# Wide attention of a block chain: the sums of four heads in one matmul visit, their reciprocals spread by ScalarE, and the output quarters a period later

## What is computed

```python
def cross_attention(x, ctx, wq, wk, wv, wo, bo):
    q, k, v = ...                       # 20 heads of 64
    scores = einsum('bhnd,bhmd->bhnm', q, k) * SCALE
    attn = softmax(scores, axis=-1)
    out = einsum('bhnm,bhmd->bhnd', attn, v)
    return einsum('bnf,fe->bne', out, wo) + bo

x = cross_attention(layer_norm(x, g1, be1), layer_norm(x, g1, be1), wq1, wk1, wv1, wo1, bo1) + x
x = cross_attention(layer_norm(x, g2, be2), context, wq2, wk2, wv2, wo2, bo2) + x
```

## Time and profile before

| | us |
|---|---|
| median of 3 runs | 3481.67 (3481.03 to 3483.08) |
| the profiled execution | 3482.07 |
| its span | 3480.3 |
| TensorE busy | 3284.0 |
| VectorE busy | 1760.0 |
| ScalarE busy | 1505.8 |
| GpSimd busy | 672.0 |
| granted clock, mean share of full | 0.985 |

### The profile page before, as it was taken

The page is one execution under the profiler, slowest core; times in us unless marked ns, Lnnn a source line. Parts: engine busy times, 40 slices in busy tenths (PEclk is TensorE's granted clock), DMA queues, the critical chain, the costliest instruction groups (busy, mean ns, idle before and its releaser), DMA issues.

```text
span 3480.3 us, 39327 instructions
## 1 busy us (share of the span) xinstructions
PE 3284.0 (94%) x15478; PEld 1478.6 (42%) x15478; DVE 1760.0 (51%) x2728; ACT 1505.8 (43%) x2023; POOL 672.0 (19%) x420
## 2 busy tenths in 40 slices
PE   7999999999999999998999899999997999989997
PEld 3434344443434343434454344444433455643443
DVE  2645455454545455562223666777771221656774
ACT  3544444444454545451111555666652111326664
POOL 2433334333334343340000000000000000000000
PEclk9999999999999999999999999999999999989999
DMA  3000000000100000002000000000003000000000
GB/s 109 20 16 19 17 16 19 22 15 22 32 16 19 16 22 13 16 7 59 0 1 25 1 1 1 22 9 7 1 1 83 0 1 22 3 5 6 5 1 31
DMA packets 43558, 60.54 MB, mean 17 GB/s; under 512 B 7408, under 2 KB 31216, under 8 KB 43376
## 3 DMA queue, kind: packets, MB, share of 16 engines
q1 hardware_dynamic: 43376, 58.02, 5.8%
HBM read 55.39 MB, written 2.62 MB: 17 GB/s over the span
## 4 chain that ended last, share of the span: by engine, by line
PE 86%; ACT 6%; DVE 5%; issue 2%; DMA 0%; POOL 0%; SPq 0%; ACTq 0%; DVEq 0%; POOLq 0%
PE bank L548 8%; PE bank L465 8%; PE bank L1027 6%; PE bank L670 5%; PE bank L350 5%; PE bank L606 4%; PE bank L1463 4%; PE bank L960 4%; PE bank L1465 4%; PE bank L1143 3%; PE bank L609 3%; PE bank L642 3%; PE bank L1466 2%; PE bank L1080 2%; PE bank L1168 2%; DVE heads L985 2%
## 5 line engine op out<-in xcount | busy, mean ns | idle before, releaser
L498 DVE TENSOR_REDUCE heads<-bank 128x2 f32<-128x1024 f32 x320 | 392.4, 1226 | 673.7 <-PE bank L487 673.7
L985 DVE TENSOR_REDUCE heads<-bank 128x1 f32<-128x512 f32 x960 | 597.9, 683 | 237.2 <-PE bank L973 236.4
L521 ACT ACTIVATE probs<-bank 128x1024 f32<-128x1024 f32 x320 | 327.7, 1024 | 130.1 <-PE bank L474 129.9
L534 POOL TENSOR_TENSOR heads<-heads,probs 128x1024 f32<-128x1024 f32 x160 | 377.1, 2357 | 12.5
L530 POOL TENSOR_TENSOR heads<-probs 128x1024 f32<-128x1024 f32 x80 | 192.4, 2405 | 931.9 <-ACT probs L521 931.9
L465 PE MATMUL bank<-heads 64*128 64x512 f32 x1280 | 335.7, 602 | 0.1
L960 PE MATMUL bank<-heads 32*128 32x512 f32 x1920 | 296.5, 628 | 25.7 <-ACT weights L998 14.9
L548 PE MATMUL bank<-probs,values 128*64 128x512 f32 x1280 | 292.3, 598 | 9.3 <-ACT heads L617 4.9
L577 DVE RECIPROCAL rec<-ox 128x128 f32<-128x128 f32 x320 | 270.2, 907 | 8.0 <-ACT ox L570 8.0
L998 ACT ACTIVATE weights<-bank 128x1024 f32<-128x1024 f32 x238 | 230.6, 1021 | 100.2 <-PE bank L960 99.6
L1487 ACT ACTIVATE probs<-bank,b_col 128x512 f32<-128x512 f32 x80 | 55.0, 687 | 455.3 <-PE bank L1466 455.3
(11 more groups left out here) (199 smaller groups left out, 4725.2 us busy)
## 6 DMA issues: line engine op xcount, KB each, us to landing
heads<-in_wqk SPq DMA_DIRECT2D x40, 320.0 KB, 2.9
heads<-in_wqk SPq DMA_DIRECT2D x40, 256.0 KB, 2.6
ctx_in<-in_ctx SPq DMA_DIRECT2D x12, 384.0 KB, 3.7
weights<-in_L_xattn_wo SPq DMA_DIRECT2D x2, 1600.0 KB, 11.7
x_res<-in_x SPq DMA_DIRECT2D x4, 640.0 KB, 12.3
out<-x_res SPq DMA_DIRECT2D x1, 2560.0 KB, 8.7
weights<-in_L_xattn_w_ff SPq DMA_DIRECT2D x1, 1600.0 KB, 12.3
weights<-in_L_xattn_ff_w SPq DMA_DIRECT2D x1, 1600.0 KB, 14.2
```

Source lines behind the costliest of these rows:

```text
L498: nc.vector.tensor_reduce(v["negm"][:, U % 2, qb, :].rearrange("p (g k) -> p g k", g=2)[:, :, 0], M.ROWS[:, :, :], AX.X, ALU.max, negate=T ...
L521: nc.scalar.activation(v["probs"][:, kb, :, :], M.COLS[kb % 2][:, :, :], ACT.Exp, scale=float(r.work[n][0].prm["dh"]) ** -0.5).then_inc(r. ...
L534: nc.gpsimd.tensor_tensor(ps, ps, pr[:, k, :, :], ALU.add).then_inc(r.sem("part"), 1)
L985: nc.vector.tensor_reduce(v["negm"][:, tile, qb, 32 * h + at:32 * h + at + 1], r.bank_of(item, m)[:, :], AX.X, ALU.max, negate=True).then_ ...
```

## The change

The sums are made once in two periods, in the odd ones. Four matmuls of 32 columns put the sums of the pair of the even period in rows 0 to 31 and 64 to 95 of the bank, those of the odd one in rows 32 to 63 and 96 to 127. ScalarE evicts this tile once, and VectorE takes its reciprocals once, in the following even period. In the odd period after that ScalarE makes two tiles of it, `rec` for the even pair and `rec_odd`, in which each sum stands in all 64 rows of its head: a copy of the whole tile, two copies of 32 rows, and when they have landed two more of 32 rows (`w_spread_act`). Then VectorE multiplies both pairs' mixes (`w_divide_dve`). Since the last division of a batch is now in period 1 of the next, the output quarters move from periods 1 to 4 to periods 2 to 5, and V2 from periods 5 and 6 to periods 0 and 1. `step_items` is changed in the same way.

```diff
@@ -176,6 +176,7 @@
+                v["rec_odd"] = M.heads[:, 9984:10496]
...
@@ -451,7 +452,7 @@
-                    items += [(f"mix{u}", n), (f"den{u}", n)]
+                    items += [(f"mix{u}", n)] + ([(f"den{u}", n)] if u % 2 else [])
...
@@ -525,7 +526,8 @@
-                r.wait_full(pool, f"den{(U - 2) % 10}", (U - 2) // 10)
+                W = U - 1 - U % 2
+                r.wait_full(pool, f"den{W % 10}", W // 10)
...
@@ -556,31 +558,50 @@
-            for g in range(2):
-                last = nc.tensor.matmul(r.bank_of(item, n)[64 * g:64 * g + 64, :], M.ones[:, :], v["psum"][:, U % 2, g, :], start=True, stop=True)
+            for e in range(2):
+                for g in range(2):
+                    at = 64 * g + 32 * e
+                    last = nc.tensor.matmul(r.bank_of(item, n)[at:at + 32, :], M.ones[:, 0:32], v["psum"][:, e, g, :], start=True, stop=True)
-            r.wait(act, "rcp", 4 * (10 * n + u))
+            r.wait(act, "rcp", 4 * ((10 * n + u) // 2))
-        def w_recip_dve(dve, r, n, u, j):
-            c = slice(j * P, j * P + P)
-            if j == 0:
-                r.wait_out(dve, f"den{u}", n)
-                r.wait(dve, "on", 10 * n + u)
-            nc.vector.reciprocal(M.rec[:, c], M.ox[:, c]).then_inc(r.sem("rcp"), 1)
-        def w_divide_dve(dve, r, n, u):
-            v, U = n_view(r, n), 10 * n + u
-            r.wait(dve, "rcp", 4 * U + 4)
-            r.wait_out(dve, f"mix{u}", n)
-            nc.vector.tensor_tensor(v["OT"][U % SLOTS], v["OT"][U % SLOTS], M.rec[:, :], ALU.mult).then_inc(r.sem("on"), 1)
+        def w_recip_dve(dve, r, U):
+            for j in range(4):
+                c = slice(j * P, j * P + P)
+                if j == 0:
+                    r.wait_out(dve, f"den{U % 10}", U // 10)
+                    r.wait(dve, "on", U - 1)
+                nc.vector.reciprocal(M.rec[:, c], M.ox[:, c]).then_inc(r.sem("rcp"), 1)
+        def w_spread_act(act, r, U):
+            odd = n_view(r, 0)["rec_odd"]
+            r.wait(act, "rcp", 4 * (U // 2 + 1))
+            nc.scalar.copy(odd[:, :], M.rec[:, :]).then_inc(r.sem("spread"), 1)
+            r.wait(act, "spread", 5 * (U // 2) + 1)
+            for a in (0, 64):
+                nc.scalar.copy(odd[a:a + 32, :], M.rec[a + 32:a + 64, :]).then_inc(r.sem("spread"), 1)
+            r.wait(act, "spread", 5 * (U // 2) + 3)
+            for a in (0, 64):
+                nc.scalar.copy(M.rec[a + 32:a + 64, :], M.rec[a:a + 32, :]).then_inc(r.sem("spread"), 1)
+        def w_divide_dve(dve, r, U):
+            r.wait(dve, "spread", 5 * (U // 2 + 1))
+            for W, rec in ((U - 1, M.rec), (U, n_view(r, 0)["rec_odd"])):
+                out = n_view(r, W // 10)["OT"][W % SLOTS]
+                r.wait_out(dve, f"mix{W % 10}", W // 10)
+                nc.vector.tensor_tensor(out, out, rec[:, :], ALU.mult).then_inc(r.sem("on"), 1)
...
@@ -743,11 +764,11 @@
-                    if u in (1, 2, 3, 4) and old:
-                        w_y_pe(pe, r, n - 1, u - 1)
-                    if u in (5, 6) and now:
-                        w_V2_pe(pe, r, n, 2 * u - 10)
-                        w_V2_pe(pe, r, n, 2 * u - 9)
+                    if u in (2, 3, 4, 5) and old:
+                        w_y_pe(pe, r, n - 1, u - 2)
+                    if u in (0, 1) and now:
+                        w_V2_pe(pe, r, n, 2 * u)
+                        w_V2_pe(pe, r, n, 2 * u + 1)
...
@@ -767,7 +788,8 @@
-                        w_den_pe(pe, r, n, u)
+                        if u % 2:
+                            w_den_pe(pe, r, n, u)
...
@@ -780,9 +802,11 @@
-                    if u in (5, 6) and now:
-                        w_V_act(act, r, n, 2 * u - 10, 2)
-                        w_V_act(act, r, n, 2 * u - 9, 2)
+                    if u % 2 and 0 <= 10 * n + u - 2 < 10 * r.N:
+                        w_spread_act(act, r, 10 * n + u - 2)
+                    if u in (0, 1) and now:
+                        w_V_act(act, r, n, 2 * u, 2)
+                        w_V_act(act, r, n, 2 * u + 1, 2)
...
@@ -803,7 +827,8 @@
-                        w_den_act(act, r, n, u)
+                        if u % 2:
+                            w_den_act(act, r, n, u)
...
@@ -816,12 +841,12 @@
-                    if 0 <= U - 1 < 10 * r.N:
-                        for j in range(4):
-                            w_recip_dve(dve, r, (U - 1) // 10, (U - 1) % 10, j)
-                        w_divide_dve(dve, r, (U - 1) // 10, (U - 1) % 10)
-                    if u in (1, 2, 3, 4) and old:
-                        w_y_dve(dve, r, n - 1, u - 1)
+                    if u % 2 == 0 and 0 <= U - 1 < 10 * r.N:
+                        w_recip_dve(dve, r, U - 1)
+                    if u % 2 and 0 <= U - 2 < 10 * r.N:
+                        w_divide_dve(dve, r, U - 2)
+                    if u in (2, 3, 4, 5) and old:
+                        w_y_dve(dve, r, n - 1, u - 2)
...
```

More of the change, by code:

```diff
@@ L438, in step_items @@
                     items += [(f"Q{w}", m), (f"K{w}", m)]
-                if u in (1, 2, 3, 4) and old:
-                    items += [(f"y{u - 1}", n - 1)]
-                if u in (5, 6) and now:
-                    items += [(f"V2_{2 * u - 10}", n), (f"V2_{2 * u - 9}", n)]
+                if u in (2, 3, 4, 5) and old:
+                    items += [(f"y{u - 2}", n - 1)]
+                if u in (0, 1) and now:
+                    items += [(f"V2_{2 * u}", n), (f"V2_{2 * u + 1}", n)]
                 if u == 7 and new:
```

## The result

| | before | after |
|---|---|---|
| median, us | 3481.35 (3477.19 to 3483.08, 4 runs) | 3538.32 (3533.82 to 3539.99, 4 runs) |
| the profiled execution, us | 3482.07 | 3537.65 |
| its span, us | 3480.3 | 3535.9 |

The ratio is 1.0163, 95% interval 1.0146 to 1.0181: 57 us slower.

What follows compares the result with a forecast made beforehand. TensorE's work was taken to count in full, ScalarE's only where something TensorE needs stands behind it. Terms summed to +25.2 us, plus 12 for the clock, giving 3519 us, range 3498 to 3540.

Steps and rivals of the forecast that it cites:

- 40 visits saved: TensorE's sums: four 32-column matmuls every second period, so 40 of 80 visits of 0.86 us go, 34.3 us less.
- tiling changes: Between mix (128x64) and sums (128x32) on TensorE: one added change of tiling, 0.10 us each, 40 times, 4.0 us more.
- period 7: T0's eviction behind the cast of K has no slack, so the copies delay it 2.9 us seven times, 20.3 us.
- period 1: V2's first eviction waits behind the copies: 2.2 us three times, 2.9 four times in cross batches, 18.2 us.
- period 9: In front of cross batches V's first eviction starts later behind the copies: 1.1 us four times, 4.4 us.
- quarters: Periods 3 and 5, batches 1 to 7: two divides delay the output quarter whose bank the mix needs, 14 x 0.55 = 7.7 us.
- clock in the wide run: TensorE's clock falls in the eleven long new pauses, 1.1 us each (between 0 and 1.7), about 12 us more.
- fourth rival: The sums' visit doesn't shrink: the four tiles queue in four slots, TensorE gains nothing, 3553 us; chance 0.03.
- third rival: ScalarE copies of 32 rows cost only a fixed 0.15 us, shift about 1.1 us: faster, 3466 us; chance 0.11.
- second rival: The copies open the summed pauses but TensorE's clock does not fall: 3507 us; chance 0.20.
- fifth rival: Waits compound: copies cost 0.65 us apiece, the clock falls at all 14 pauses by 1.7 us: 3537 us; chance 0.14.
- first case: As summed: the copies open pauses in TensorE's work and the clock falls in them, 3519 us; chance 0.48.

Runs made afterwards that it cites:

- filled kernel: The changed kernel with spare float32 matmuls in TensorE's pauses ahead of negm, in periods 7 and 1: 3516.56 us, ratio 1.01 against the kernel before.
- one copy: The changed kernel with the spread cut to its first copy of 128 rows, the four of 32 rows left out: 3463.35 us, ratio 0.9948 against the kernel before.
- moves alone: The kernel before with only V2 moved to periods 0 and 1 and the output quarters to 2 to 5: 3482.31 us, ratio 1.000.
- copies alone: The kernel before plus five unused ScalarE copies in each odd period, where the change puts its spread: 3559.65 us against 3482.38, ratio 1.0222.
- three copies: The changed kernel without the last two copies of the spread: 3491.16 us, ratio 1.0028 against the kernel before.

## Why the forecast held, and where it fell short

The table sets the forecast's terms beside what the periods measure. A period's length is the time from its first exp to the next period's. The clock is taken out by reading lengths where the clock is up (in the filled kernel, for periods 7 and 1), and 0.14 us of tiling is taken off the odd ones.

| term | forecast | measured | from |
|---|---|---|---|
| 40 visits saved | -34.3 | -34.4 | plain even period 15.23 before, 14.37 after |
| tiling changes | +4.0 | +5.6 | 0.14 each: odd period without waits 15.37, one copy |
| period 7 | +20.3 | +22.5 | 7 x 3.22 (21.25 - 17.89 - 0.14) |
| period 1 | +18.2 | +19.8 | 3 x 2.42 and 4 x 3.13 |
| period 9 | +4.4 | +5.6 | 4 x 1.39 (23.54 - 22.01 - 0.14) |
| quarters | +7.7 | +4.5 | 6 x 0.26 and 8 x 0.37 |
| plain odd periods | +1.2 | +2.3 | 3 x 0.77 (16.14 - 15.23 - 0.14) |
| the end, idle | +3.7 | +3.8 | 8.76 - 4.93 |
| sum | +25.2 | +29.7 | |
| clock in the wide run | +12 | +23 | the 79 periods together are 49.0 longer, of which the terms above explain 25.8 |

With 0.7 us of clock at the end that makes 53.4 of the 55.6 us between the spans. The other 2 us are the balance of two parts that the change doesn't touch. The first exp of the wide run starts 1.6 us earlier (57.5, before 59.1), and the stretch from the feed-forward's first matmul to the end takes 1876.7 us in place of 1872.3. With the moves alone it takes 1868.9, so it scatters by as much from execution to execution.

- **What bounds** was read rightly: TensorE's work counted in full (0.86 per visit), ScalarE's by what stood behind it. The copies alone, the moves alone and the one copy separate the two and come within 2 us of their sums, which were made with the shift from the changed kernel's trace; three copies came inside the band that was expected for a falling clock.
- **Four tiles side by side** held, by the 42.7 us of the sums, and so the fourth rival fell. The change of tiling costs 0.14, not 0.10: the mix to the sums takes 3.59 us from start to start (312.57 to 316.16) instead of 3.48, and some hundredths more behind them. The Trainium skill (TensorEngine Tiling (Array Packing), Key Properties) has it that a changed mode drains the array; the trace agrees, with this price.
- **The copies** were taken at a shift of 2.9 us and took 3.20, near the bound of 3.25 that stood beside it. The step that was off is the 0.53 us between independent instructions, read from a cast of 128 rows and its follower. It holds for a float32 copy of 128 rows (0.52 in the one-copy run), but whatever comes behind a copy of 32 rows starts 0.64 later, and four of the five copies are such. The third rival, copies that cost less with fewer rows, fell: 615 ns for 32 rows, 613 for 128.
- **The quarters** were overpriced: a divide was taken at 0.86, the value beside GpSimd's additions, and takes 0.69 here. GpSimd's last addition has ended by then, at 307.6 with the first divide at 310.82.
- **The clock** is the term that was mis-sized most: 1.1 us for eleven pauses were assumed, 23 us came. Three things were off. Behind four of the seven longest pauses the half clock lasts 6.8 us (6.7 of them in the stretches above), and TensorE works for 5.4 of them, where the row that the forecast went by had 3.25; periods 7 lost 0.9 to 2.3 us, 12.0 in sum. In periods 1 of batches 6 and 7 it cost 2.8 and 3.0, and nothing in batches 4 and 5, where the pauses are as long (3.01). And in period 9, where the sum had no clock, a pause of 1.22 us among other short ones took 1.6 us in three of four batches. The second rival, no clock at all, fell with the stretches at 0.50: the clock is 23 of the 57 us.
- **The fifth rival**, to which the forecast gave 0.14, has the measured time, 3537, and is nearer in both its terms than the case that was forecast: 0.65 apiece for the copies (0.64 measured) and 24 us for the clock (23). It is right in part by luck: the clock did not fall at all 14 pauses by 1.7 us but at nine of them, by 0.9 to 3.0, and at three of period 9 that no case had. The first case, with 0.48, was right in kind and short in size, mostly by the clock (11 us of the 19), the shift of the copies (0.3 us at each place) and the tiling (1.6); the quarters' 3 us too much worked the other way.

## What to carry to other kernels

An engine's idle share does not tell whether work put on it is free: the same five copies cost 77 us behind the cast of K and nothing one period earlier, on an engine that is under half busy. Look for the instruction behind the new one in the queue and for who waits for it; with banks that are shared in turn that is the group two further on. And where TensorE is the bound, price each new pause with the clock that it may cost, which was four tenths of the loss here and came behind pauses down to 1.2 us, or fill it.

## What the runs showed of the hardware that was not expected

- Pauses decide over the clock only loosely: 3.89 us of idle was followed by half clock 7 times of 7 in the changed kernel, 2.60 us 4 of 7 with three copies, 2.30 us in neither of two cases in the changed kernel but in three of four with the copies alone, and 1.19 us in 3 of 7 with one copy. Which one it is can't be told from the length of the pause alone.
- In the version with the spread in the even period VectorE divides while GpSimd adds, and its divides of 128x512 take 1.86 and 2.85 us (rows above) where they take 0.69 in the changed kernel; the reciprocals, with one input from SBUF, stay at 0.90 us. Each such divide ends 0.55 us after the GpSimd addition that it met (260.84 and 260.29, 419.23 and 418.68); in the kernel before, where a divide started just ahead of an addition's end, it was the same 0.55 (224.62 and 224.07), which made its 0.86. GpSimd waits too: most of its additions take 2.35 us, but 38 that start before a held-up divide has ended take 2.70, so that two in a row take 5.11 (rows above) in place of 4.78. The Trainium skill (SBUF — State Buffer, SBUF: two separate sides) describes a port pair that VectorE, with two SBUF inputs, and GpSimd hold in turn for a whole instruction; the trace agrees, with these waits on both sides. Nothing waits for these divides, so it costs no time here.
- A ScalarE copy of 32 rows is as long as one of 128 (615 and 613 ns), but what follows it starts 0.64 us after its start even where it doesn't wait for the copy, and behind the one of 128 rows 0.52. The copies of 32 rows also move their rows to other rows, and no run tells whether this or the number of rows makes the difference.
